# One signal per PSUM bank in the last block's gated MLP, and the second half's residual and norm ahead of its sixth and seventh products

## What is computed

```python
x = x + h * g_msa
h = _ln(x) * (1 + sc_mca) + sh_mca
h = _topk_cross_attn(h, context, w_q, b_q, w_kv, b_kv, w_co, b_co)
x = x + h * g_mca
h = _ln(x) * (1 + sc_mlp) + sh_mlp
u = h @ w_m1 + b_m1
a, b = (u[..., :HID], u[..., HID:])
h = silu(a) * b @ w_m2 + b_m2
x = x + h * g_mlp
```

## Time and profile before

| | us |
|---|---|
| median of 3 runs | 1655.57 |
| lowest and highest run | 1642.3 and 1657.22 |
| the profiled execution | 1649.2 |
| its span, from the first to the last instruction | 1647.4 |
| TensorE busy | 1538.9 (93%) |
| VectorE busy | 1050.7 (64%) |
| ScalarE busy | 771.2 (47%) |
| GpSimd busy | 379.2 (23%) |
| mean granted clock of TensorE | 0.981 |

### The profile page before, as it was taken

One profiled execution on the slowest core, in us unless ns is written; L12 is line 12 of the kernel. 1 busy time (PEld: TensorE's weight loads), 2 busy tenths in 40 slices (PEclk: granted clock), 3 DMA queues, 4 the chain that ended last, 5 costly groups with the idle time before them and its releaser, 6 DMA issues.

```text
span 1647.4 us, 26630 instructions
## 1 busy us (share of the span) xinstructions
PE 1538.9 (93%) x10605; PEld 939.2 (57%) x10605; DVE 1050.7 (64%) x2954; ACT 771.2 (47%) x1232; POOL 379.2 (23%) x419
## 2 busy tenths in 40 slices
PE   5899999999999999988999999999999999997898
PEld 3456675444454857656765657543444475665676
DVE  3573345999727446799357434589991744579953
ACT  1434421688853533325443543148886354333544
POOL 3420006342016000114133000534310701001320
PEclk9999999999999999999999999999999999999999
DMA  9500018121020000000130000732202000000000
GB/s 338 147 1 0 0 33 172 26 37 26 2 78 1 1 0 2 2 1 1 42 125 1 1 1 0 178 35 40 40 2 78 1 0 1 2 2 1 1 1 26
DMA packets 37552, 59.62 MB, mean 36 GB/s; under 512 B 7360, under 2 KB 26980, under 8 KB 36532
## 3 DMA queue, kind: packets, MB, share of 16 engines
q1 hardware_dynamic: 25239, 34.71, 6.4%
q0 software_dynamic: 9408, 15.85, 6.0%
q10 hardware_dynamic: 2780, 7.36, 1.3%
HBM read 42.03 MB, written 2.10 MB: 27 GB/s over the span
## 4 chain that ended last, share of the span: by engine, by line
PE 66%; DVE 22%; issue 6%; ACT 3%; DMA 1%; POOL 1%; ACTq 0%; DVEq 0%; POOLq 0%
PE ps L1001 9%; PE ps L1013 9%; PE ps L464 5%; PE ps L1321 4%; PE ps L986 3%; PE ps L875 3%; DVE taken L2382 3%; PE ps L1114 3%; PE ps L592 2%; DVE taken L2394 2%; DVE rs L2064 2%; DVE mxw L2056 2%; PE ps L853 2%; PE ps L1105 2%; DVE m L2377 2%
## 5 line engine op out<-in xcount | busy, mean ns | idle before, releaser
L2249 DVE TENSOR_REDUCE mm<-ps 128x1 f32<-128x1024 f32 x256 | 310.5, 1223 | 35.1 <-PE ps L986 31.5
L1642 ACT ACTIVATE pt<-ps 128x512 f32<-128x512 f32 x512 | 276.8, 599 | 60.9 <-PE ps L1001 42.9
L2500 POOL TENSOR_TENSOR rstd<-ve,minus_half 128x4 f32<-128x4 f32 x32 | 35.7, 1116 | 740.3 <-DVE ve L1928 740.3
L1001 PE MATMUL ps<-qx,kx 64*128 64x512 f32 x512 | 188.3, 445 | 1.0 <-ACT pt L1642 1.0
L986 PE MATMUL ps<-kx,qx 48*128 48x512 f32 x512 | 186.6, 444 | 0.2
L1013 PE MATMUL ps<-pt,v 128*32 128x256 f32 x2048 | 158.7, 390 | 0.0
L1001 PEld LDWEIGHTS ps<-qx,kx 64*128 64x128 f32 x512 | 78.9, 184 | 96.0 <-ACT pt L1642 85.9
L592 PE MATMUL ps<-filler 128*128 128x512 f32 x382 | 117.3, 432 | 0.0
L2139 DVE TENSOR_TENSOR rlo<-ring,rhi 128x512 fp32r<-128x512 f32 x48 | 33.2, 692 | 120.9 <-ACT ring L1592 120.9
L1013 PEld LDWEIGHTS ps<-pt,v 128*32 128x32 f32 x2048 | 42.9, 108 | 85.6 <-ACT pt L1642 61.9
L986 PEld LDWEIGHTS ps<-kx,qx 48*128 48x128 f32 x512 | 75.4, 184 | 24.4 <-issue 19.7
(11 more groups left out here) (375 smaller groups left out, 3377.0 us busy)
## 6 DMA issues: line engine op xcount, KB each, us to landing
wm<-in_L_xcond_W_mlp_dram SPq DMA_DIRECT2D x4, 1024.0 KB, 7.9
qx<-q_hi POOLq DMA_DIRECT2D x64, 64.0 KB, 2.4
kx<-k_hi POOLq DMA_DIRECT2D x64, 64.0 KB, 2.5
w3a<-in_L_xcond_w_m_dram SPq DMA_DIRECT2D x2, 2048.0 KB, 7.6
w<-in_L_xcond_e_w_dram SPq DMA_DIRECT2D x6, 512.0 KB, 7.7
w<-in_L_xcond_e_w_dram SPq DMA_DIRECT2D x2, 1536.0 KB, 14.8
s_ada<-in_L_xcond_w_ada_dram ACTq DMA_DIRECT2D x1, 2304.0 KB, 22.5
qx<-q_lo POOLq DMA_DIRECT2D x32, 64.0 KB, 2.4
```

Source lines behind the costliest of these rows:

```text
L1001: pe.matmul(ps[:, bank, :], kx[r, p % 4, kc * P:(kc + 1) * P], qx[r, p % 4, half * 512:(half + 1) * 512], start=True, stop=True).then_inc( ...
L1642: act.activation(pt[:, u % 8, half * 512:(half + 1) * 512], ps[:, bank, :], ACT.Exp, scale=QK_SCALE).then_inc(st_read, 1)
L2249: return dve.tensor_reduce(mm[:, p % 2, e, t:t + 1], place(), X, ALU.max).then_inc(ring_read, 1)
```

## The change

Three edits go together. First, Silu of bank 4 increments `h3_read` too, so the semaphore counts 2 for each product; `up(n)` waits ahead of the gate matmuls for the gate of n-1 to be read, and ahead of the up matmuls for the up part of n-1 to be read. Other readers' counts are doubled. Second, on TensorE `down(5)` and `ln(7, 1)` stand ahead of `up(7)`, and on ScalarE the norm's evictions ahead of `hidden(7)`. Third, on VectorE the residual add and statistics of half 1 stand ahead of `times(5)`, `xhat` ahead of `times(6)`, and `hTlo` ahead of `times(7)`.

```diff
-                    def halves(terms, inc, each=False):
+                    def halves(terms, inc, each=False, first=True):
                         for i in range(2):
+                            if n and first:
+                                pe.wait_ge(h3_read, 2 * (n0 + n) - 1 + i)
...
                     if n == 0:
                         pe.wait_ge(w3_split, b * 3 + 3)
-                    else:
-                        pe.wait_ge(h3_read, n0 + n)
                     if m == 0:
                         halves(TERMS[0:2], False, True)
                         pe.wait_ge(hs3_lo[k], b + 1)
-                        halves(TERMS[2:], True)
+                        halves(TERMS[2:], True, first=False)
...
                 up(5)
                 up(6)
-                up(7)
                 down(5)
                 ln(7, 1, 2)
+                up(7)
                 down(6)
...
-                    act.activation(gate3[k][:, m % 4, :], ps[:, 4, :], ACT.Silu, bias=colT[:, C_BM13 + m:C_BM13 + m + 1])
+                    act.activation(gate3[k][:, m % 4, :], ps[:, 4, :], ACT.Silu, bias=colT[:, C_BM13 + m:C_BM13 + m + 1]).then_inc(h3_read, 1)
...
                 product_hi(6)
+                ln(7, 1, (mod, M3_SC_ML, M3_SH_ML), 2)
                 hidden(7)
                 product_hi(7)
-                ln(7, 1, (mod, M3_SC_ML, M3_SH_ML), 2)
...
-                    dve.wait_ge(h3_read, n0 + n + 1)
+                    dve.wait_ge(h3_read, 2 * (n0 + n) + 2)
...
                 divide(7)
+                add(1, 0)
                 times(5)
-                add(1, 0)
                 product_lo(5)
+                normalise(b, 7, 1)
                 times(6)
-                normalise(b, 7, 1)
                 product_lo(6)
+                tokens3_lo(1)
                 times(7)
                 product_lo(7)
-                tokens3_lo(1)
```

More of the change, by code:

```diff
@@ L1423, in _ @@
                         elif n == 2 * NC_HID + 1:
-                            pe.wait_ge(h3_read, n0 + 2 * NC_HID)
+                            pe.wait_ge(h3_read, 2 * (n0 + 2 * NC_HID))
                             ln(0, 1, 4, b + 1)
@@ L2631, in times @@
                 def times(n):
-                    pool.wait_ge(h3_read, n0 + n + 1)
+                    pool.wait_ge(h3_read, 2 * (n0 + n) + 2)
                     pool.tensor_tensor(gate3[0][:, n % 4, :], gate3[0][:, n % 4, :], up3[0][:, n % 4, :], ALU.mult).then_inc(prod_pool, 1)
```

## The result

| | before | changed |
|---|---|---|
| median of 8 runs, us | 1649.11 | 1633.98 |
| lowest and highest run, us | 1641.81 and 1657.22 | 1630.42 and 1639.75 |
| profiled execution, us | 1649.2 | 1639.75 |
| its mean granted clock | 0.981 | 0.981 |

The ratio is 0.9918 with a 95% interval of 0.9892 to 0.9944: 13.5 us faster, 9.2 to 17.8 (the two medians of the table lie 15.1 us apart, the two means 15.0). The forecast was 8.1 us, and the clock rival's upper side 15. The profiled execution of the changed kernel, which has the same mean clock as that of before, is 9.5 us shorter, and it is the slowest of its eight runs. The forecast time was 1644 in a range of 1633 to 1654; the median, 1633.98, lies just inside its lower end. So there are two things to explain: the 8 to 9 us in the traces, and what comes on top in the runs.

What follows compares the result with a forecast made beforehand. TensorE, busy 93% of the span, was taken as the bound. 2 x (3.75 + 0.3) = 8.1 us gain; 1652.4 - 8.1 gave 1644 us, in a range of 1633 to 1654.

Steps and rivals of the forecast that it cites:

- the clock rival: Whole kernel: clock dips, 1.8 us each, added or removed; four would make the gain 1 us, or 15; chance 0.11.
- The four waits: TensorE idles 0.78 us before `up(6)`, `up(7)`, `up(10)` and 0.71 inside `up(8)`; together worth 4.09 us per batch.
- What a stall costs (0.78 idle = 1.04 us): TensorE before `up(6)`, `up(7)`, `up(10)`: 0.78 idle, 0.16 drain and 0.10 slower first pair make 1.04 us.
- the `hTlo` wait: TensorE inside `up(8)`, released by VectorE: 0.71 us idle plus 0.26, 0.97 us per batch, expected to go.
- `affine` and Silu ready in time at `up(6)` and `up(10)`: ScalarE's evictions precede TensorE's need, so both waits go; Silu(9), behind two `yT` evictions, is covered by 0.5 us.
- The new wait before `down(5)`, 0.34 us: TensorE after `up(6)`: `down(5)`, covered by one product instead of two, waits 0.24 + 0.10 us per batch.
- the sum: One batch, second projection to product 10: 4.09 of stalls less 0.34 of new wait gives 3.75 us.
- VectorE's cover: Residual add to variance fits VectorE's wait ahead of `times(5)`, with 0.1 to 0.4 us left.
- The thin cover ahead of `up(8)`, 0.65 us: Silu(7), behind the norm on ScalarE, ends at 809.0; `up(8)` wants it at 809.65.
- The tail of the top-k stage, 0.3 us a batch: `up(4)` waits only for Silu(3) and starts earlier; gain 0.3 us per batch, between 0 and 0.6.
- the base: Middle of the four times of the kernel before, 1652.4 us, from which the 8.1 us gain was taken.

Runs made afterwards that it cites:

- The new orders alone: Kernel before with only the changed orders on TensorE, ScalarE and VectorE, one wait for both banks: ratio 0.9967, 5.0 us less at equal clock.
- the delayed norm: Changed kernel with ScalarE's first eviction of the half 1 norm done three times in a row: 2.3 us over the changed kernel by the distances.
- the single halves: Kernel before with only the separate signal for each bank, ratio 0.9974, and with only the new orders, ratio 0.9967.
- the single batches: The whole change in one batch, the other as in the kernel before: batch 0 alone ratio 0.9936, batch 1 alone 0.9969.
- the kernels with added matmuls: Useless matmuls: changed kernel, 18 in batch 0 or 1; kernel before, 18 in batch 0; changed, 9 in batch 0: 4.12, 4.13, 4.11, 2.08 us over by distances.
- one signal alone: Kernel before with only the separate signal for each bank, all orders as before: ratio 0.9974, 4.9 us less at equal clock.

## Why the prediction came out as it did

**Where TensorE waits, and that both batches repeat it: right.** The four waits were all of it but 0.17 us (below); all four are gone in both batches.

**What a stall costs (0.78 idle = 1.04 us): right.** The new orders alone removed one such stall and the `hTlo` wait, worked out at 2.01 us, and measured 2.08; to the 0.07 between them belong the 0.17 below and a new hold of 0.12 at `up(8)`, where Silu(7) and `affine(7)` stand behind the norm.

**`affine` and Silu ready in time at `up(6)` and `up(10)`: right.** Silu(9), behind the two `yT` evictions, did not hold `up(10)`.

**The new wait before `down(5)`, 0.34 us: right in place, 0.38 by the rows** (802.54 - 802.26, and 0.10 for the first matmul).

**What the sum missed: 0.17 us a batch.** The start of `up(8)` was itself held by the `hs` eviction before, which the trace shows as idle time of the weight loads and not of the matmuls, and I read only the latter. The row of the weight loads in the kernel before:

```profile
811.58 0.19 PEld L1321 LDWEIGHTS ps<-hs,w3a_hi 128*128 128x128 f32 x1 [0.34 <-ACT hs L1436]
```

The first pair starts at 811.29 and the next at 811.92, 0.63 apart instead of 0.46. 4.09 + 0.17 - 0.38 = 3.88, against 3.91.

**VectorE's cover: there, as forecast, but put too small.** I started the residual add at the projection's end. It waits for one bank at a time, and the add starts 0.9 us before the projection's end; it began at 796.04 and the cover was 0.75 us, not 0.1 to 0.4. GpSimd's `rstd` took 1.01 us, not 1.38.

**The thin cover ahead of `up(8)`, 0.65 us: right.** 0.62 by the trace, 0.57 by the delayed norm.

**The tail of the top-k stage, 0.3 us a batch: right,** 0.37 to 0.40 by the traces (`top_turn(5)` to the projection, 33.30 us in the kernel before and 32.91 in the changed one in batch 0); `up(4)` started without a wait at 783.27.

So the stretches give 2 x (3.91 + 0.4) = 8.6 us for 8.1 forecast, and the mechanism of the forecast is shown. What fell short is the last step, that these are all and that the clock is an even gamble on top of them (a chance of 0.11). The first runs gained 13.5 us, nearer to the upper side of that rival (15) than to 8.1. The mean clock rose from 0.9813 (95 runs) to 0.9849 (15 runs), which at 1.14 us for 0.001 is 4.1 us. With the change in batch 1 alone it stayed (0.9814), with it in batch 0 alone it rose (0.9857), and 2.1 us of added work in batch 0 took it away (0.9807). That the clock goes with the kernel is shown by this; the cause is not, and neither is it that the sign could have been forecast. I had priced this rival rightly in size (some 1.8 us a dip, a handful of dips) and taken its sign for chance. What stands in the earlier trace rows, which I read as agreeing that the clock varies from run to run, are two places in one execution and can't show it; that the same stretch has another clock in another execution is shown below.

The median of before on which I leaned was of three runs, 1655.57; over eight it was 1649.11. The forecast time of 1644 was 10 us above the result. 3.3 us of that are the base, 1652.4 against 1649.11, and the rest is the gain, 15.1 by the medians against 8.1. That the result is inside the range is owed to the width of the range, which the scatter of three runs gave it: with the median of eight runs for a base the forecast would have been 1641.

**What stays open.** At equal clock the changed kernel is 10.1 us under the kernel before, give or take 0.6, where the traces have 8.6; the single halves and the single batches too read 0.5 to 0.8 us more than their distances and the tail, and the kernels with added matmuls between 0.1 less and 0.9 more. The mean clock is a figure of the whole span: 0.001 of 1640 us is 1.6 us, and the slope is 1.14, so part of the lost clock costs nothing. In which stages is not shown, so the slope is a mixture; I can't say whether that is all of it. Nor is it shown which of batch 1's stages gain. Some dips lie ahead of every edit: the stretch of the earlier trace rows, at 0.91 in the trace of before, reads in the changed kernel

```profile
600.00:620.00 20.00, 18.41 (x156) 10.23 (x151) 10.68 (x12) 6.98 (x9) 3.38 (x2) 1.00 0.00 1
```

and 0.91 again in the trace with the change in batch 0 alone: it varies from one execution to the next.

## What to carry to other kernels

Where two PSUM banks are filled and read in turn, count each bank's release by itself: the wait for the second reader was worth 1.04 us each time that nothing else stood between, and the added increments and waits show no cost (twelve matmuls take 2.79 us before and 2.78 after). Removing a stall brings TensorE earlier to the next chain, so move that chain's first links (here a residual add into 9 us of waiting time on VectorE) in the same edit; either half alone gave 1.7 to 2.1 us a batch, both 3.9. And look at the granted clock of many runs, and at stretches ahead of the edit, before the rest of a gain is given to the edit: the kernel with 2.1 us of added work ran 6.5 us longer (1642.6 against 1636.1, in different groups) and was 2.08 us longer by its distance.

## What was not expected of the hardware

The mean granted clock differs between kernels by more than their runs scatter: 0.9862 +-0.0016 and 0.9807 +-0.0008 on one chip for two programs that differ by 18 matmuls near the end against 9 in the middle. The stretches into which the matmuls were put ran at clock 1.00.

The Trainium skill (TensorE: Matmul & The Clock Gate, What's actually happening) says that the monitor's window runs freely and does not start with the kernel. By that alone a shift of batch 1 should change which runs meet a dip and leave their mean; the runs show a mean that differs, and twelve runs that scatter over 0.979 to 0.984 only, where the kernel before scatters over 0.975 to 0.989. Why is open.

GpSimd's `rstd` operation on 128 x 4 took 1.01 us where VectorE stood still for its first 0.7 us, behind the statistics, and 1.38 us where VectorE worked beside it all the time. So it is in the other traces: 1.38 with the old orders (one signal alone, and batch 0 of the kernel with the change in batch 1 alone), 1.01 with the new ones. That VectorE's work is the cause is not shown.
